# Local heads' values and routing-weight rows fetched by DMA from DRAM instead of being spread by matmuls

## What is computed

```python
xn = layernorm(x)
q, k, v = split(xn @ w_qkv + b_qkv)                      # 16 heads of 8
ctx[:, :4] = softmax(q k^T / sqrt(8), causal) @ v        # "global" heads
ctx[:, 4:] = softmax(q k^T / sqrt(8), window of 32) @ v  # "local" heads
s  = ctx @ w_out + b_out
cw = top-4 of 16 sigmoid scores within 2 of 4 groups, normalised, times 2.5
y  = sum_e cw[n, e] * (silu(xn Wg_e^T) * (xn Wu_e^T)) @ Wd_e^T  + shared expert
out = x + s * silu(xn + y)
```

## Time and profile before

| | |
|---|---|
| median of 3 runs | 536.37 us (535.66 to 537.6) |
| the profiled execution | 535.39 us, of which the span of the profile is 533.6 us |
| PE busy | 479.1 us, 90% |
| DVE, ACT, POOL busy | 347.8, 329.1, 269.0 us |
| mean busy share of the DMA engines (SP's queue) | 30.4% |
| from one batch to the next | 122.9 us (the step `cw` starts at 156.42, 279.21 and 402.15 us) |

### The profile page before, as it was taken

The page is one execution under the profiler, slowest core; times in us unless marked ns, Lnnn a source line. Parts: engine busy times, 40 slices in busy tenths (PEclk is TensorE's granted clock), DMA queues, the critical chain, the costliest instruction groups (busy, mean ns, idle before and its releaser), DMA issues.

```text
span 533.6 us, 10570 instructions
## 1 busy us (share of the span) xinstructions
PE 479.1 (90%) x3832; PEld 286.6 (54%) x3832; DVE 347.8 (65%) x755; ACT 329.1 (62%) x654; POOL 269.0 (50%) x239
## 2 busy tenths in 40 slices
PE   1859978899999989899999988999999998989995
PEld 0647554555446755555446765545546765544442
DVE  7876439775977638776787546776788532676414
ACT  3536753767956554666957556475976566366972
POOL 3407942265737852254655872145664963016623
PEclk9979999999999999999999999999999999899998
DMA  9275374000450575000350387000170178000001
GB/s 214 79 177 100 57 99 66 1 1 2 121 77 1 164 97 78 1 1 1 116 83 1 93 153 94 2 1 1 32 159 9 40 125 133 4 2 0 1 1 39
DMA packets 144077, 32.37 MB, mean 61 GB/s; under 512 B 120966, under 2 KB 136346, under 8 KB 144026
## 3 DMA queue, kind: packets, MB, share of 16 engines
q1 hardware_dynamic: 143696, 31.41, 30.4%
q10 hardware_dynamic: 330, 0.30, 0.3%
HBM read 22.25 MB, written 9.44 MB: 59 GB/s over the span
## 4 chain that ended last, share of the span: by engine, by line
PE 56%; DVE 13%; ACT 8%; issue 7%; SPq 6%; POOL 3%; DMA 3%; DVEq 2%; POOLq 1%; ACTq 0%
PE bank L791 8%; PE bank L739 6%; PE bank L708 5%; PE bank L678 5%; PE bank L572 4%; SPq L536 4%; PE bank L574 4%; PE bank L573 4%; PE bank L755 3%; ACT stage L936 2%; DVE mxp L1176 2%; DMA kall<-planes 2%; PE bank L646 2%; PE bank L779 2%; PE bank L715 2%
## 5 line engine op out<-in xcount | busy, mean ns | idle before, releaser
L936 ACT ACTIVATE stage<-bank 128x512 f32<-128x512 f32 (+3 forms) x240 | 112.7, 539 | 59.2 <-PE bank L712 27.9
L1253 POOL TENSOR_TENSOR wrow<-wrow,gates 128x512 f32<-128x512 f32 x64 | 82.5, 1289 | 90.6 <-ACT wrow L865 90.0
L1176 DVE TENSOR_REDUCE mxp<-bank 128x1 f32<-128x512 f32 (+4 forms) x192 | 89.8, 516 | 23.7 <-PE bank L681 14.2
L1262 POOL TENSOR_TENSOR hid<-hid,wrow 128x512 f32<-128x512 f32 x64 | 82.4, 1287 | 28.4 <-DVE hid L1140 23.5
L1245 POOL TENSOR_TENSOR maxd<-mxp,k 128x512 f16<-128x512 f32 x32 | 34.7, 1083 | 95.9 <-DVE mxp L1178 51.2
L791 PE MATMUL bank<-hid,down_w 128*128 128x512 f32 x144 | 76.0, 618 | 0.0
L1140 DVE SCALAR_TENSOR_TENSOR hid<-hid,bank 128x512 f32<-128x512 f32 x72 | 48.7, 677 | 39.5 <-PE bank L574 28.6
L854 ACT ACTIVATE hid<-bank 128x512 f32<-128x512 f32 x72 | 43.7, 606 | 44.2 <-PE bank L574 44.2
L1178 DVE TENSOR_REDUCE mxp<-bank 128x8 f32<-128x512 f32 x48 | 30.9, 686 | 49.3 <-PE bank L690 49.0
L678 PE MATMUL bank<-kall,qpad 128*128 128x512 f16 (+4 forms) x192 | 52.2, 320 | 10.6 <-DVE mxp L1176 3.7
L572 PE MATMUL bank<-xh,up_hi 128*128 128x512 f32 x144 | 58.7, 408 | 2.0 <-DVE hid L1140 1.2
(11 more groups left out here) (158 smaller groups left out, 907.7 us busy)
## 6 DMA issues: line engine op xcount, KB each, us to landing
planes<-qkh SPq DMA_DIRECT2D x16, 256.0 KB, 3.2
qtmp<-planes SPq DMA_DIRECT2D x16, 256.0 KB, 3.2
kall<-planes SPq DMA_DIRECT2D x16, 256.0 KB, 3.5
qpad<-planes SPq DMA_DIRECT2D x128, 32.0 KB, 2.8
kpad<-planes SPq DMA_DIRECT2D x48, 64.0 KB, 3.3
xin<-in_L_attn_x_dram SPq DMA_DIRECT2D x4, 512.0 KB, 4.5
planes<-qkl SPq DMA_DIRECT2D x8, 256.0 KB, 3.4
xres<-in_L_attn_x_dram SPq DMA_DIRECT2D x4, 512.0 KB, 3.7
```

What stands on the lines that cost most here:

```text
L936: act.activation(prob[:, t % NPROB, 0:cols], ps[:, 0:cols], ACT.Exp).then_inc(freed, 1)
L1176: ins = dve.tensor_reduce(mxp[:, c, j:j + 1], ps[:, 0:cols], AX_X, ALU.max)
L1253: pool.tensor_tensor(row, row, gates[:], ALU.mult).then_inc(gated, 1)
L1262: pool.tensor_tensor(hid[:, i % NHID, :], hid[:, i % NHID, :], wrow[:, (EP * c + t) % NWT, :] if t < EP else gates[:], ALU.mult)\
```

## The change

The rows of weights and the values no longer go through PE. `cwT` is stored to DRAM (`cw_rows`, scaled by 0.5), and each `wrow` tile is loaded from there by two DMAs that repeat one row of 2 KB over 64 partitions. There are six buffers; six tiles are loaded behind the second `cwT` of a batch, and each of the other ten at the `down` step whose buffer comes free. `vn` is stored to DRAM (`v_rows`), and one step `v` loads `vbd` by twelve DMAs (3 groups x 4 heads), each of 32 x 32 pieces of 8 floats. The matmuls, the ACT copies, the DVE masks and the high and low parts are gone; the zeros of `vbd` are written once. The ring of three banks now holds two tiles per `up` step. The three order strings are new.

```diff
-NWT = 3
+NWT = 6
+            def load_weights(n):
+                c, t = n // EP, n % EP
+                for side in range(2):
+                    sp.dma_start(wrow[I * side:I * (side + 1), n % NWT, :],
+                                 cw_rows[2 * t + side:2 * t + side + 1, chunk(c)].broadcast_to([I, CH])).then_inc(wrow_loaded[n % NWT], 16)
...
+                    elif kind == "vn":
+                        sp.wait_ge(emptied[at.bank(s)], at.taken(s))
+                        if at.next:
+                            sp.wait_ge(v_loaded, 16 * 4 * GLOBAL * at.next)
+                        sp.dma_start(v_rows.rearrange("(t p) d -> p t d", p=P)[:, TPC * c:TPC * (c + 1), :],
+                                     vn[:, TPC * c:TPC * (c + 1), :]).then_inc(v_stored, 16)
+                    elif kind == "v":
...
+                            sp.wait_ge(pv_done, b * SCORES_BEFORE[HG] + SCORES_BEFORE[GLOBAL])
+                        sp.wait_ge(v_stored, 16 * NCH * (at.next + 1))
+                        for g in range(GLOBAL):
+                            for h in range(4):
+                                own = slice(HD * h, HD * (h + 1))
+                                sp.dma_start(vbd[BLK * h:BLK * (h + 1), :, g, own],
+                                             v_rows[:, BLK * g:BLK * (g + 1)][:, own].rearrange("(j k) d -> k j d", k=BLK))                                    .then_inc(v_loaded, 16)
+                    elif kind == "cwT":
+                        sp.wait_ge(emptied[at.bank(s)], at.taken(s))
+                        sp.dma_start(cw_rows[:, chunk(c)], cwT[:, chunk(c)]).then_inc(cw_rows_stored, 16)
+                        if c == NCH - 1:
+                            sp.wait_ge(cw_rows_stored, 16 * NCH * (at.next + 1))
...
+                            for n in range(NWT):
+                                load_weights(n)
+                    elif kind == "down" and s[2] < EP:
+                        n = EP * c + t + NWT
+                        if n < NCH * EP:
+                            sp.wait_ge(hid_ready, at.of(s) * NCH * NUP + (NUP * c + t + 1))
+                            load_weights(n)
...
-                    elif kind == "v":
-                        pe.matmul(used, repeat[:, i, :], vn_hi[:].rearrange("p t d -> p (t d)"), start=True, stop=False)
-                        done(at, s, pe.matmul(used, repeat[:, i, :], vn_lo[:].rearrange("p t d -> p (t d)"), start=False, stop=True))
...
+                        if g == 0 and n == 1:
+                            pe.wait_ge(v_loaded, 16 * 4 * GLOBAL * (b + 1))
...
-                                done(at, s + (x,), pe.matmul(ps[:], pairsel[:, t, :], cwT[:, chunk(c)], start=True, stop=True))
...
-                            act.activation(wrow[:, iw % NWT, :], banks[at.bank(weight)][:], ACT.Copy)\
...
-                        pool.wait_ge(emptied[at.bank(weight)], at.taken(weight))
+                        pool.wait_ge(wrow_loaded[n % NWT], 2 * 16 * (at.of(s) * LOADS_OF[n % NWT] + n // NWT + 1))
```

117 lines of the change are left out of this document (49 added, 68 removed).

## The result

The changed kernel takes **564.33 us** (median, 561.45 to 567.49) against 536.54 for the kernel before: ratio 1.051, 95% interval 1.048 to 1.054, so it is 5% slower. The forecast was 543.7 with a range of 519 to 562: the direction was its likeliest one, the size was not, and the result lies above the range. The profiled execution took 561.45 us with a span of 559.6; before, the span was 533.6. The 26.0 us between the spans are what is explained here.

The account below looks back on a forecast made before the run. PE, 90% busy, was taken as the bound, except from seam to third group, where loads run neck and neck. Start +5.3, three batches +0.8 each, LAST -0.4: +7.3 on 535.4 gives 542.7, median 543.7; range 519 to 562.

Parts of the forecast that it names:

- The double cost: Rival: half-size vbd pieces cost double at the seams, 16 us for twelve loads, +8 a seam, 576 us; chance 0.10.
- The relief: Rival: PE keeps the time freed by removed passes, since loads are cheap and global-stage waits shrink; 520 us, chance 0.27.
- The clock: Rival: PE's wait at group 1's first max tile lowers the clock, +1.5 us at four seams, 550 us; chance 0.13.
- The late `wrow`: A wrow reload lands too late behind SP's other waits and POOL waits: 0 to 2 us a batch; no separate chance.
- (1): Profile sign: 128 passes gone from PE, its busy time lower by more than 26 us.
- (2): Profile sign: SP issues a vbd load in 0.66 us; under 0.4 favours the relief, over 1.2 the double cost.
- (3): Profile sign: PE idle 4 to 6 us before group 1's first max tile in each batch, ended by kall or qpad.
- (4): Profile sign: the first max tile of group 1 in batch 0 comes at about 71 us.
- (5): Profile sign: batches stand 123.5 to 124 us apart.
- (6): Profile sign: DMA share digits of 7 to 9 in a longer run of slices at each seam.
- (7): Profile sign: clock digits under 9 at the seams, if the clock falls.
- (8): Profile sign: POOL's wait for wrow, in front of L1253's line, is ended by a DMA and not by ACT.

Follow-up runs that it names:

- best placement: Changed kernel with the vbd loads moved to the middle of the batch before and, in FIRST, ahead of group 0's strips: 541.2 us.
- ACT's queue: Changed kernel with the ten wrow reloads of each batch issued by ACT instead of SP: 563.2 us, against 564.3.
- the repaired wait: Kernel before, with group 1's strips and pads waiting for their real last readers instead of qfull 0,0: 532.9 us, ratio 0.992.

## Why the prediction was wrong

The forecast's mechanism is what happened: "the time of PE that is freed is spent in front of a longer queue of loads". What failed is the size of its terms, the price of a tile of rows above all. In the order in which it gave them, for the first seam:

| term | forecast | measured |
|---|---|---|
| `cwT` to `up 0,0` | 6.9 | 174.86 - 168.63 = 6.2 |
| to SP's first issue behind the store | 5.9 | 181.97 - 174.86 = 7.1 |
| one tile of rows | 0.85 | 1.85 |
| twelve `vbd` loads | 8.0 | 8.75 |
| two tiles | 1.7 | 2.98 |
| `xin`, `xres` | 0.9 | 1.3 |
| strips to the first `max` tile | 8.1 | 8.3 |
| group 1 to group 3 | 20.6 | 226.49 - 205.18 = 21.3 |
| group 3 to the next `cwT` | 70.8 | 71.0 |

1. **The step that failed is the price of a tile of rows.** I took 0.85 us, worked out from the data (256 KB at 324 GB/s), and said that SP "needs about as long for its two issues". No row showed that: the rows have 0.34 to 0.66 for one load, so two are 0.7 to 1.3, and 0.85 is near the low end. Measured: 597 ns in the median for each of 128, 1.2 to 1.5 us a tile, in the row above 1.85. A batch has 16 tiles, so this is some 6 us of SP's time. The three tiles of the seam came 2.3 us dearer, the nine at the start 3.8; with the first seam taken for all three, that is an estimated 11 of the 19 us by which the profiled execution (561.45) lies above its forecast (542.7).
2. **The second is an item left out.** The seam's sum starts behind the last `outT` and takes SP to be free there. SP was behind: the first six tiles take it until 179.53 us (7.5 us, again more than 5.1), and the two stores of `vn` (1.1 us) stand between them and the stores of the output. The piece from `up 0,0` to SP's first issue behind the store was 7.1 us for 5.9.
3. **The start** was forecast at 71.3 and came at 76.43. The routing came as said (stores at 35.68, forecast 35.7). The landing of the stores took 2.4 instead of 3.2, the six tiles 7.6 instead of 5.1, the next tile 1.2 instead of 0.85, the later tiles, `xin` and `xres` 4.0 instead of 2.6, `vbd` 8.75 instead of 8.0, and the strips to the tile 8.9 instead of 8.1.
4. **The price of a `vbd` load** was sound: 569 ns in the median (530 to 1314), 0.73 in the mean, for 0.66. The rule of the Trainium skill in "DMA: Bandwidth & Descriptors", section "Why small descriptors are slow (HBM only)", by which 32 bytes cost 4 where 64 cost 5, is neither shown nor refuted: it is about packets, and the medians (569 for 32 bytes, 664 ns for 64) are SP's time to issue. The twelve loads, an estimated 6.4 us by it, took 8.7. The double cost (1.34 us a load) is ruled out.
5. **The relief** did come where no load stood in the way, but it is small: 0.6 us of 71.6 behind group 3, forecast 0.8; LAST was 1.0 shorter from its first `max` tile on, forecast 0.4.
6. **The clock** fell as the rival said, to 0.67 in the window of the stall. The Trainium skill, "TensorE: Matmul & The Clock Gate", section "HAM oscillation — how this bites in real kernels", describes such falls behind waits for DMA; the trace agrees on the fall. But the 6 us that I gave it are not there: with the clock held at 1.00 through that window the time was the same (565.6).
7. **The late `wrow`** cost next to nothing, 2.4 us of POOL's waits in all; POOL waits for ACT's copy of the gates now (59.9 us).

Of the signs listed, (1) was wrong in size and in its reason (10.8 us of busy time, not over 26: the page's total counts an overlap once, since PE's groups of the kernel before add up to 711 us and its total is 479.1; and the passes that stayed got longer, those of L616 by 11.7 us, at a mean granted clock of 0.942 for 0.988), (2) was 0.57 to 0.73, (3) was right in kind with 6.5 to 11.1 us instead of 4 to 6, (4) was 5 us late, (5) 127.4 and 128.9 instead of 124, (6) and (7) came true, and (8) did not: of POOL's 62.2 us ahead of `wrow`, ACT's copy of the gates ends 59.9.

That the loss is one of place and length of SP's queue is shown by the runs: 541.2 us with the same loads and the whole computation, placed elsewhere. What sets the queue's length is shown for the rows (SP's time to issue, at a share of 0.58) and not for `vbd`, where the share is 0.79 to 0.85 and SP's issues and the engines' work were not told apart. That the change is worth having even so is not shown: with its best placement, ACT's queue and the repaired wait it takes 532.9 us, as the kernel before does with that repair alone. Its first half, the rows, with the values by matmul, ACT's queue and the repaired wait, takes 528.8. It is faster than the kernel before, but so is the repair alone. The two were measured on different chips, and their intervals to the kernel before overlap (0.980 to 0.990, 0.989 to 0.995), so that the rows by DMA are worth the 4 us between the two is likely rather than shown.

## What to carry to other kernels

Count what a new load costs on the queue that issues it (here 0.6 us for each, whatever its 32 to 128 KB) beside what its data cost the DMA engines; where it is issued in a stretch that is full already, take it out of there first. An engine that is 90% busy is not the bound of the stretch in which it waits: a pass removed there is worth nothing until the wait is. When an edit that must shorten a queue gives nothing, look at what the queue waits for next: here SP stood idle for 3 to 11 us behind a stand-in for the real last readers, and that wait had cost the kernel before 0.8%, of which its trace shows 2.3 us in the first batch.
